# Decoder layer, second phase: turning the normalised tokens by VectorE blocks and transfers inside SBUF instead of TensorE transpositions

## The chip, the cores and the metric

One NeuronCore of a Trainium2 chip runs the whole program. It has five engines with queues of their own: TensorE (PE, and PEld for its weight loads), VectorE (DVE), ScalarE (ACT), GpSimd (POOL) and SyncE (SP), which here issues nearly all transfers. Engines wait for each other by semaphores only, and each works through its queue in order. The metric is the device time of one execution in microseconds; less is better.

## What is computed

Tokens are 4096 rows (16 sequences of 256) of 256 features. Three layers follow each other, each a sublayer, a residual sum and a layer norm:

```
x = _layernorm(x + attn(x, ...), axis=-1)           # first phase
x = _layernorm(x + xattn(x, ctx, ctx, ...), axis=-1)  # second phase
x = _layernorm(x + ffn(x, ...), axis=-1)            # third phase
```

The second one, which the change touches, is a differential attention over the context with 16 heads of 16 features:

```
s1 = einsum('bshe,bthe->bhst', q1, k1) / scale ;  s2 = einsum('bshe,bthe->bhst', q2, k2) / scale
attn = softmax(s1) - gain * softmax(s2)
o = einsum('bhst,bthe->bshe', attn, vp) ; o = (o - mean) / sqrt(var + EPS)
out = o.reshape(B, S, D) @ wo.T
```

where q1 and q2 are linear in the normalised tokens x. The queries therefore need x with features on partitions, while the first phase leaves it in X1 with tokens on partitions.

## The kernel before

All matrices are 32-bit floats. Where precision matters a value is split into a high and a low part.

**Blocks.** `phase_b` handles the tokens in 8 groups p of 512 (two sequences) and each group in two halves c of 128 features (8 heads). One such half is a block B = 2p + c; there are 16 (`NB`). A block has two units u = 2B + b, one per sequence; there are 32 (`NU`). A unit takes eight steps s, two for each of the four pairs of heads i, so there are 256 steps (`NS`), of which 16 make a block. Preparations run ahead: steps start at -52, beside the end of phase a.

**One step on TensorE** (`step` in `tensor`, L1340): `maxima(s + 14)`, the raw scores of a unit 14 steps ahead, whose maximum VectorE takes (L1495, one reduction a step); `scores(s)`, the same scores again with rows of minus maximum added through four extra partitions; on even steps `values`, the product with the values; and then what `due` puts on that step: `rows` (L1239) turns the maxima, `turn_o` (L1277) and `turn_n` (L1285) turn outputs, `prep_k` and `prep_v` make keys and values of later blocks, `prep_x` (L1209) turns tokens. `scores(s)` waits until ScalarE has done exp of the step before (`act_ex`), since it writes the same banks P[4] and P[5].

**How x is turned.** `prep_x(B)` at step 16B - 41 makes four 128x128 transpositions of X1 into bank P[6]. A step later ScalarE copies the bank to the tile XF (L1407), and a step later GpSimd makes XS from XF by three instructions: the high part, the low part, the high part again (L1631 to L1635).

**Transfers.** SP's queue runs through the same steps. `load(B, i)` (L1100), at steps 16B - 23 + 3i, i = 0 to 3, brings the heads' keys from KS to KT and queries from XS to QT: 2 transfers of each, so 16 in a block. `put_maxima(u)` (L1120), at step 8u - 4, brings the turned maxima from NR into QT with two transfers; `scores` of step 8u waits for them through `d_mr`. `load_ctx` brings context for two blocks. Modulo 16, the steps on SP are: 9 load i = 0; 12 put_maxima, load_ctx, load i = 1; 15 load i = 2; 2 load i = 3; 4 put_maxima. All transfers go through the helper `dma` (L118, shown as L119).

The order of the work is fixed by these step numbers; nothing is chosen while it runs.

Of the kernel before, what the change touches and what calls it, by code (L numbers as in the profile page):

```python
# [6 lines left out]
ALU = mybir.AluOpType  # L7
# [90 lines left out]
def due(step, first, every, count):  # L98

    k, r = divmod(step - first, every)  # L100
    return k if r == 0 and 0 <= k < count else None


def f32(ap):
    return ap.bitcast(F32)
# [12 lines left out]
def dma(e, o, i, sem):  # L118
    e.dma_start(o, i).then_inc(sem, 16)  # L119
# [759 lines left out]


LEAD = 14
NU = 4 * NP
NB = 2 * NP
NS = 8 * NU
# [5 lines left out]
def phase_b(M, a_end):  # L890
    nc, a, P, PP, X1, ident, nhalf = M.nc, M.a, M.P, M.PP, M.X1, M.ident, M.nhalf
    put = Place(M, 0)
# [4 lines left out]
    XF = put("XF", [128, TOK])  # L897
# [17 lines left out]
    put = Place(M, M.spare)  # L915
# [12 lines left out]
    ZR = put("ZR", [128, 2, 4, 2])  # L928
    VM = put("VM", [128, 16])
    VR = put("VR", [128, 16])  # L930
    BN = put("BNb", [128, 4, 6])
    AG = put("AGb", [128, 4, 2])
    RS = put("RSb", [128, 4])
# [25 lines left out]
    d_cr = M.sem("b_cr")  # L959
    d_ld = [[M.sem(f"b_ld{i}_{h}") for h in range(4)] for i in range(2)]  # L960
    d_mr = [M.sem(f"b_mr{i}") for i in range(2)]
    d_T = M.sem("b_T")
    d_V = M.sem("b_V")
    pe_g = M.sem("b_pe_g")
# [13 lines left out]
    act_x = M.sem("b_act_x")  # L978
# [14 lines left out]
    dve_oh = M.sem("b_dve_oh")  # L993
    dve_x2 = M.sem("b_dve_x2")
    dve_ag = M.sem("b_dve_ag")
    dve_fold = M.sem("b_dve_fold")
    dve_seq = M.dve_seq
    pool_vt = M.sem("b_pool_vt")
# [2 lines left out]
    pool_xs = M.sem("b_pool_xs")  # L1001
# [29 lines left out]

    def x_due(s):
        return due(s, -41, 16, NB)

    def v_due(s):
        for i, at in enumerate((-17, -7, -3, -1)):
# [32 lines left out]
    def turn_n_due(s):  # L1069
        return due(s, 23, 8, NU)  # L1070

# [11 lines left out]
    def sync(e):  # L1083
        w = Passed(e)

        def load_ctx(p):
            w.wait_ge(pool_c, 4 * p)
            dma(e, CR[:, :, :], ctxT[:, :, p * TOK:(p + 1) * TOK], d_cr)

        def ones_rows(i):  # L1090
            w.wait_ge(dve_w, 5)
            if i:
                after(w, "w2")
            else:
                after_stack(w, 14)
            for g in range(2):
                dma(e, f32(KT[i][64 * g + 48:64 * g + 52, :, :, :]).rearrange("r i m t -> r i (m t)"),
                    f32(ones[:, :, :]).rearrange("r m t -> r (m t)").unsqueeze(1).to_broadcast([4, 4, 1024]), d_ones)

        def load(B, i):  # L1100
            p, c = B // 2, B % 2
            if B == 0:
                after_stack(w, 14)
                w.wait_ge(dve_w, 4)
                w.wait_ge(pe_g, 1)
            if B == 1:
                after(w, "w2")
            w.wait_ge(pool_ks, 2 * B + 2)
            w.wait_ge(dve_ks, 2 * B + 2)
            w.wait_ge(pe_st, 16 * (B - 2) + 8 + 2 * i + 2)  # L1110
            k, q = KT[B % 2], QT[B % 2]
            for g in range(2):
                h = 2 * i + g
                dma(e, f32(k[64 * g:64 * g + 48, i, :, :]).rearrange("r m t -> r (m t)"),
                    f32(KS[16 * h:16 * h + 16, c, :, :, :]).rearrange("d l m t -> d (l m t)"), d_ld[B % 2][i])
                if B:
                    w.wait_ge(pool_xs, 3 * B + 3)
                    dma(e, f32(q[64 * g:64 * g + 48, i, :, :]).rearrange("r b t -> r (b t)"), f32(XS[16 * h:16 * h + 16, c, :, :]), d_ld[B % 2][i])

        def put_maxima(u):  # L1120
            q, b = QT[u // 2 % 2], u % 2
            w.wait_ge(act_nr, u + 1)
            w.wait_ge(pe_st, 8 * (u - 4) + 8)
            for g in range(2):
                dma(e, f32(q[64 * g + 48:64 * g + 52, :, b, :]), f32(NR[u % 2][16 * g:16 * g + 16, :]), d_mr[u % 2])

        def load_fold():
            for i in range(4):
                w.wait_ge(d_ld[0][i], 64 * NP)
                w.wait_ge(d_ld[1][i], 64 * NP)  # L1130
            w.wait_ge(pe_v, 4 * NP)
            for name in T:
                dma(e, T[name], a[name].rearrange("(c p) n -> p c n", c=2), d_T)
            w.wait_ge(d_ones, 80)
            for o, name in ((vb, "vb"), (vc, "vc"), (v2, "v2"), (br[:, :, :], "br"), (cols[:, :], "cols")):
                dma(e, o, a[name], d_V)
            dma(e, BC[:, 0, :], a["BC"][:, 0, :], d_V)

        def first_queries():
            w.wait_ge(dve_w, 4)  # L1140
            w.wait_ge(pe_g, 1)
            w.wait_ge(pool_xs, 3)
            for i in range(4):
                for g in range(2):
                    h = 2 * i + g
                    dma(e, f32(QT[0][64 * g:64 * g + 48, i, :, :]).rearrange("r b t -> r (b t)"), f32(XS[16 * h:16 * h + 16, 0, :, :]), d_ld[0][i])

        def first(i):
            if i == 0:
                load_ctx(0)  # L1150
            elif i == 1:
                dma(e, bd[:, :, :, :], a["bdw"], d_w)
            else:
                dma(e, wor[:, :, :], a["xwoT"].rearrange("(c p) n -> p c n", c=2), d_w)
                dma(e, kones[:, :], a["kones"], d_ones)

        def step(s):
            if s == -33:
                first_queries()
            u = due(s, -4, 8, NU)  # L1160
            if u is not None:
                put_maxima(u)
            p = ctx_due(s)
            if p is not None:
                load_ctx(p)
            for i in range(4):
                B = due(s, 3 * i - 23, 16, NB)
                if B is not None:
                    load(B, i)
            for i, at in enumerate((-16, -6)):  # L1170
                if s == at:
                    ones_rows(i)
            if s == NS - 28:
                load_fold()

        return first, step

    def tensor(e):
        w = Passed(e)
# [160 lines left out]
        def step(s):  # L1340
            busy(BUSY.get(s, 0))
            if 0 <= s + LEAD < NS:
                maxima(s + LEAD)
            if s in (0, 1):
                busy(2, 4 + 2 * s)
            if 0 <= s < NS:
                scores(s)
            v = values_due(s)
            if v is not None:
                values(v)  # L1350
            u = rows_due(s)
            if u is not None:
                rows(u)
            o = turn_o_due(s)
            if o is not None:
                turn_o(*o)
            u = turn_n_due(s)
            if u is not None:
                turn_n(u)
            k = k_due(s)  # L1360
            if k is not None:
                prep_k(*k)
            B = x_due(s)
            if B is not None:
                prep_x(B)
            v = v_due(s)
            if v is not None:
                prep_v(*v)
            o = out_due(s)
            if o is not None:  # L1370
                output(*o)
            f = fold_due(s)
            if f is not None:
                fold(f)
# [3 lines left out]
    def scalar(e):  # L1378
        w = Passed(e)
# [10 lines left out]
        def step(s):  # L1390
            v = values_due(s - 1)
# [9 lines left out]
                w.wait_ge(d_mr[u % 2], 32 * (u // 2))  # L1401
                e.activation(NR[u % 2][:, :], low[0:32, :], ACT.Copy).then_inc(act_nr, 1)
            B = x_due(s - 1)
            if B is not None:
                w.wait_ge(pe_x, B + 1)
                w.wait_ge(pool_xs, 3 * B)
                e.activation(XF[:, :], P[6], ACT.Copy).then_inc(act_x, 1)  # L1407
            v = v_due(s - 1)
            if v is not None:
                p, i = v  # L1410
# [5 lines left out]
            if u is not None:  # L1416
                p, c, b = u // 4, u // 2 % 2, u % 2
# [4 lines left out]
            k = k_due(s - 1)  # L1422
            if k is not None:
                B, m = k
# [17 lines left out]
    def vector(e):  # L1442
        w = Passed(e)
# [28 lines left out]
        def step(s):  # L1472
            o = out_due(s - 1)
            if o is not None:
                p, b, halves = o
# [43 lines left out]
            if s == -26:  # L1519
                w.wait_ge(d_ones, 16)  # L1520
                e.tensor_copy(ones[:, :, :], kones[:, :].unsqueeze(2).to_broadcast([4, 2, TOK])).then_inc(dve_w, 1)
            u = turn_n_due(s - 1)
            if u is not None:
                c, b = u // 2 % 2, u % 2
# [53 lines left out]
    def gpsimd(e):  # L1578
# [27 lines left out]
        def step(s):  # L1606
# [16 lines left out]
            B = x_due(s - 2)  # L1623
            if B is not None:
                xs = XS[:, B % 2, :, :]
                w.wait_ge(act_x, B + 1)
                for i in range(4):
                    w.wait_ge(d_ld[B % 2][i], 64 * ((B - 2) // 2 + 1))
                after_stack(w, 13)
                one.wait()  # L1630
                one.done(e.tensor_copy(xs[:, 0, :], XF[:, :]), pool_xs)  # L1631
                one.wait()
                one.done(e.tensor_tensor(xs[:, 1, :], XF[:, :], f32(xs[:, 0, :]), ALU.subtract), pool_xs)
                one.wait()
                one.done(e.tensor_copy(xs[:, 2, :], f32(xs[:, 0, :])), pool_xs)  # L1635
            u = due(s, 11, 8, NU)
# [931 lines left out]
```

## Time and profile before

| | us |
|---|---|
| median of 3 runs | 1552.7 |
| lowest, highest | 1552.16, 1553.82 |
| span of the profiled execution | 1550.1 |
| TensorE busy in it | 1502.6 (97%) |
| VectorE, ScalarE, GpSimd busy | 1139.4, 847.5, 372.8 |

The profile shows one execution. The first phase fills it to about 350 us, the second one, between about 350 and 820 us, is the one in question, and the third follows. The span is 2.6 us below the median of the times. Times in rows are counted from the span's start. A matmul's own duration is modelled, and matmuls overlap, so the distance between the starts of two rows says what TensorE spent on the first. The clock column (PEclk) is the granted share of TensorE's 2.4 GHz: 0.50 is its other level, 1.2 GHz. A row of SP is the time that it took to issue a transfer, not the transfer.

### The profile page before, as it was taken

How to read it: one execution, taken by the hardware profiler on the slowest of the kernel's cores; microseconds unless marked ns; L12 is line 12 of the kernel's file. 1: busy time of each engine (PE TensorE's matmuls, PEld its weight loads, DVE VectorE, ACT ScalarE, POOL GpSimd, SP SyncE). 2: the span in 40 equal slices, each digit the busy share in tenths (PEclk: the TensorE clock that was granted, in tenths of full speed). 3: DMA queues.
4: the chain of work that ended last, by engine and by line, in shares of the span. 5: the costliest groups of instructions: out<-in, count | busy, mean ns of one | idle time of the engine just before them, and what ended most of it. 6: DMA issues, size and time to landing. Idle time of an engine off the chain costs nothing.

```text
span 1550.1 us, 28824 instructions
## 1 busy us (share of the span) xinstructions
PE 1502.6 (97%) x11288; PEld 1065.1 (69%) x11288; DVE 1139.4 (74%) x2305; ACT 847.5 (55%) x1123; POOL 372.8 (24%) x404
## 2 busy tenths in 40 slices
PE   8999999899999999999999999999999999999998
PEld 4333333335566666666656898888989898888887
DVE  6445555548799999999967877777676767777675
ACT  5888889876688888888863421222222221222221
POOL 1000000124556667666453300000000000000000
PEclk9999999999899999999999999999999999999999
DMA  7656665446565666657652100000000000000000
GB/s 153 137 112 117 122 121 103 71 95 113 95 93 88 105 89 98 110 78 96 93 169 69 62 1 15 1 14 1 1 15 1 14 1 15 1 15 1 1 14 14
DMA packets 61576, 97.37 MB, mean 63 GB/s; under 512 B 12461, under 2 KB 29881, under 8 KB 61441
## 3 DMA queue, kind: packets, MB, share of 16 engines
q1 hardware_dynamic: 61312, 95.34, 33.3%
q8 instruction: 89, 1.46, 0.4%
q14 instruction: 47, 0.38, 0.1%
q10 hardware_dynamic: 128, 0.20, 0.0%
HBM read 26.29 MB, written 4.19 MB: 20 GB/s over the span
## 4 chain that ended last, share of the span: by engine, by line
PE 84%; DVE 8%; ACT 3%; SPq 3%; issue 2%; DMA 1%; POOLq 0%; DVEq 0%; POOL 0%; ACTq 0%
PE ps L109 79%; SPq L119 3%; PE ps L1277 2%; DVE NM L1495 2%; ACT H L614 1%; ACT PX L1438 1%; DVE EE L758 1%; PE ps L1239 1%; DVE XC L2106 1%; PE ps L1285 1%; PE ps L1914 0%; DMA ST<-QS 0%; PE ps L1905 0%; PE ps L1209 0%; DVE QS L678 0%
## 5 line engine op out<-in xcount | busy, mean ns | idle before, releaser
L1495 DVE TENSOR_REDUCE NM<-ps 128x4 f32<-128x1024 f32 x256 | 307.5, 1219 | 29.2 <-PE ps L109 27.7
L1438 ACT ACTIVATE PX<-ps 128x1024 f32<-128x1024 f32 x256 | 262.2, 1024 | 80.2 <-PE ps L109 79.0
L614 ACT ACTIVATE H<-ps,b1c 128x1024 f32<-128x1024 f32 x256 | 268.2, 1118 | 48.6 <-PE ps L109 47.0
L2066 ACT ACTIVATE GF<-ps,cols 128x512 f32<-128x512 f32 x128 | 88.2, 689 | 295.7 <-PE ps L109 295.6
L109 PE MATMUL ps<-XC,W_sw_w 128*128 128x512 f32 x768 | 185.8, 393 | 0.0
L2257 DVE CAST GH<-GF 128x512 fp32r<-128x512 f32 x192 | 82.0, 427 | 106.9 <-ACT GF L2066 101.8
L109 PEld LDWEIGHTS ps<-XC,W_sw_w 128*128 128x128 f32 x768 | 140.5, 188 | 28.0
L2365 POOL TENSOR_SCALAR RSc<-AGc 128x4 f32<-128x4 f32 x23 | 6.9, 298 | 599.5 <-DVE AGc L2152 599.5
L109 PE MATMUL ps<-PX,VT 128*32 128x256 f32 x2048 | 138.6, 388 | 0.1
L2259 DVE TENSOR_TENSOR GH<-GF,GH 128x512 fp32r<-128x512 f32 x192 | 133.2, 694 | 6.6
L109 PE MATMUL ps<-KT,QT 48*128 48x512 f32 x512 | 128.1, 498 | 3.7 <-DVE NM L1495 1.8
L2061 ACT ACTIVATE GF<-ps 128x512 f32<-128x512 f32 x64 | 38.0, 596 | 169.2 <-PE ps L109 169.2
L109 PE MATMUL ps<-H,w2p 128*32 128x512 f32 x1024 | 124.8, 605 | 3.0 <-ACT XF L1407 1.1
L109 PE MATMUL ps<-QT,KT 52*128 52x256 f32 x1024 | 109.2, 290 | 4.7 <-ACT PX L1438 3.8
L109 PEld LDWEIGHTS ps<-QT,KT 52*128 52x128 f32 x1024 | 90.1, 187 | 26.1 <-ACT PX L1438 10.7
L109 PE MATMUL ps<-W_ml_w,GH 128*128 128x256 f32 x768 | 103.6, 285 | 0.2
L758 DVE TENSOR_SCALAR EE<-ps,b2p 128x512 f32<-128x512 f32 x63 | 47.1, 747 | 77.0 <-PE ps L109 76.9
L109 PEld LDWEIGHTS ps<-KT,QT 48*128 48x128 f32 x512 | 47.8, 184 | 80.7 <-issue 60.2
L109 PEld LDWEIGHTS ps<-W_sw_w,GH 128*128 128x128 f32 x768 | 100.0, 191 | 4.5
L109 PE MATMUL ps<-W_sw_w,GH 128*128 128x256 f32 x768 | 102.7, 283 | 0.0
L109 PEld LDWEIGHTS ps<-W_ml_w,GH 128*128 128x128 f32 x768 | 98.0, 191 | 5.8 <-issue 3.4
L109 PE MATMUL ps<-ST,w1s 48*128 48x512 f32 x512 | 96.5, 451 | 5.3 <-ACT H L614 2.0
(240 smaller groups left out, 2560.3 us busy)
## 6 DMA issues: line engine op xcount, KB each, us to landing
KT<-KS SPq DMA_DIRECT2D x128, 192.0 KB, 4.7
ST<-QS SPq DMA_DIRECT2D x254, 96.0 KB, 2.8
QT<-XSb SPq DMA_DIRECT2D x128, 96.0 KB, 4.2
XT<-in_xT_dram SPq DMA_DIRECT2D x8, 512.0 KB, 4.1
raw_a<-in_x_dram SPq DMA_DIRECT2D x8, 512.0 KB, 4.3
CR<-in_ctxT_dram SPq DMA_DIRECT2D x8, 512.0 KB, 4.7
out_dram<-X SPq DMA_DIRECT2D x7, 512.0 KB, 2.9
R_sw_w<-in_sw_w_dram SPq DMA_DIRECT2D x6, 512.0 KB, 5.5
```

What stands on the lines that cost most here:

```text
L109: return e.matmul(o, l, r, start=start, stop=stop, skip_group_check=True)
L119: e.dma_start(o, i).then_inc(sem, 16)
L614: e.activation(H1[s % 8][:, :, :], PP[s % 3][:, :, :], ACT.Tanh, bias=b1c[:, half:half + 1], scale=1.0).then_inc(act_th, 1)
L758: e.tensor_scalar(EE[:, j % 4, :], P[6][:, :], b2p[:, 0:1], None, ALU.add).then_inc(dve_ee, 1)
L1239: t = e.transpose(low[0:32, 128 * qc:128 * qc + 128], f32(NS2[u % 2][:, 4 * qc:4 * qc + 4, :, :]).rearrange("p g l n -> p (g l n)"), ident)
L1277: t = e.transpose(P[7][:, 256 * qc + 128 * i:256 * qc + 128 * i + 128], OT[f][:, i, 128 * qc:128 * qc + 128], ident)
L1438: e.activation(PX[s % 3][:, :, :, :], PP[2][:, :, :].rearrange("p g (c q) -> p g c q", c=2), ACT.Exp, bias=0.0, scale=0.25).then_inc(act_e ...
L1495: e.tensor_reduce(NM[u % 2][:, qc, :, :, i], PP[qc][:, :, :].rearrange("p g (m k) -> p g m k", m=2), AX.X, ALU.max, negate=True).then_inc( ...
L2061: e.activation(g[:, :], o, ACT.Silu, bias=0.0, scale=1.0).then_inc(act_g, 1)
L2066: e.activation(g[:, :], o, f, bias=cols[:, col:col + 1], scale=1.0).then_inc(act_g, 1)
L2257: e.tensor_copy(h[:, 0, :], g[:, :]).then_inc(dve_h, 1)
L2259: e.tensor_tensor(h[:, 1, :], g[:, :], f32(h[:, 0, :]), ALU.subtract).then_inc(dve_h, 1)
```

## The change

For blocks 0 and 1 nothing changes (`X_FIRST` = 2). For blocks 2 to 15:

- TensorE's four transpositions and ScalarE's copy of the bank to XF go.
- VectorE, at step 16B - 50, turns the 32x32 blocks of the 128 features of four token tiles in one instruction, from X1 to a new tile TX of 128 x 512. It waits for the transfers that read TX the time before.
- A turned 32x32 block still sits at the wrong place. Four groups a of four transfers, at steps 16B - 48 + a on SP, each carry 32 partitions x 512 bytes (16 KB) from TX to their place in XF; that is 16 transfers for a block. The first one waits for VectorE's instruction and for GpSimd's last reading of XF.
- GpSimd waits for them instead of for ScalarE, and reads XF with the token order unpicked (four dimensions in place of one). It makes the same three instructions.
- A scratch buffer that this program doesn't use is set to 1024 bytes, which makes room for TX.

```
+            k = turn_x_due(s)                      # vector: due(s, 16 * X_FIRST - 50, 16, NB - X_FIRST)
+            if k is not None:
+                p, c = (k + X_FIRST) // 2, (k + X_FIRST) % 2
+                w.wait_ge(*a_end["nrm"](p))
+                w.wait_ge(d_xf, 256 * k)
+                e.transpose(TX[:, :, :, :].rearrange("p b v t -> p v b t"),
+                            X1[:, 4 * p:4 * p + 4, 128 * c:128 * c + 128].rearrange("p v (b t) -> p v b t", b=4)).then_inc(dve_xt, 1)
...
+        def turn_x(k, a):                          # sync
+            w.wait_ge(dve_xt, k + 1)
+            w.wait_ge(pool_xs, 3 * (k + X_FIRST))
+            for b in range(4):
+                dma(e, XF[32 * b:32 * b + 32, 128 * a:128 * a + 128], TX[32 * a:32 * a + 32, b, :, :].rearrange("p v t -> p (v t)"), d_xf)
...
+            for a in range(4):                     # sync, in step, behind the loads
+                k = turn_x_due(s - 2 - a)
+                if k is not None:
+                    turn_x(k, a)
...
             B = x_due(s)                           # tensor; scalar the same with s - 1
-            if B is not None:
+            if B is not None and B < X_FIRST:
                 prep_x(B)
...
-                w.wait_ge(act_x, B + 1)            # gpsimd
+                xf, hi, lo = XF[:, :], xs[:, 0, :], xs[:, 1, :]
+                if B < X_FIRST:
+                    w.wait_ge(act_x, B + 1)
+                else:
+                    w.wait_ge(d_xf, 256 * (B - X_FIRST + 1))
+                    xf = xf.rearrange("p (a v t) -> p a v t", a=4, v=4)
+                    hi, lo = (ap.rearrange("p (v a t) -> p a v t", v=4, a=4) for ap in (hi, lo))
...
-                one.done(e.tensor_copy(xs[:, 0, :], XF[:, :]), pool_xs)
+                one.done(e.tensor_copy(hi, xf), pool_xs)
...
-                one.done(e.tensor_tensor(xs[:, 1, :], XF[:, :], f32(xs[:, 0, :]), ALU.subtract), pool_xs)
+                one.done(e.tensor_tensor(lo, xf, f32(hi), ALU.subtract), pool_xs)
```

SP's queue in the middle of the phase, between steps 15 and 4 modulo 16, before (KT and QT are the destinations of the loads, NR the turned maxima; the first row is the start of load i = 2):

```order
L119 DMA KT<-KS 48x1x1024 [waits b_pe_st]
L119 DMA QT<-XSb 48x1x512
L119 DMA KT<-KS 48x1x1024
L119 DMA QT<-XSb 48x1x512
L119 DMA KT<-KS 48x1x1024 [waits b_pe_st]
L119 DMA QT<-XSb 48x1x512
L119 DMA KT<-KS 48x1x1024
L119 DMA QT<-XSb 48x1x512
L119 DMA QT<-NR 4x4x256 [waits b_act_nr]
L119 DMA QT<-NR 4x4x256
```

And the same stretch now:

```order
L119 DMA KT<-KS 48x1x1024 [waits b_pe_st]
L119 DMA QT<-XSb 48x1x512
L119 DMA KT<-KS 48x1x1024
L119 DMA QT<-XSb 48x1x512
L119 DMA XF<-TXb 32x128 [waits b_pool_xs,b_dve_xt]
L119 DMA XF<-TXb 32x128 x7
L119 DMA KT<-KS 48x1x1024 [waits b_pe_st]
L119 DMA QT<-XSb 48x1x512
L119 DMA KT<-KS 48x1x1024
L119 DMA QT<-XSb 48x1x512
L119 DMA XF<-TXb 32x128 x8
L119 DMA QT<-NR 4x4x256 [waits b_act_nr]
```

Sixteen transfers now stand in front of put_maxima, eight of them also in front of load i = 3.

TensorE's queue at steps 7 and 8 modulo 16, before (C holds the identity matrix; the maxima of step 8 are KT,QT, its scores QT,KT):

```order
L1285 MATMUL ps<-C,ON 128x128 [waits b_dve_pr,b_pool_on]
L1285 MATMUL ps<-C,ON 128x128
L1209 MATMUL ps<-C,X 128x128 [waits b_act_ot]
L1209 MATMUL ps<-C,X 128x128 x3
L109 MATMUL ps<-KT,QT 128x512 [waits b_dve_red,b_ld1_3]
L109 MATMUL ps<-KT,QT 128x512
L109 MATMUL ps<-QT,KT 128x256 [waits b_act_ex,b_mr1]
```

And now:

```order
L1304 MATMUL ps<-C,ON 128x128 [waits b_dve_pr,b_pool_on]
L1304 MATMUL ps<-C,ON 128x128
L109 MATMUL ps<-KT,QT 128x512 [waits b_dve_red,b_ld1_3]
L109 MATMUL ps<-KT,QT 128x512
L109 MATMUL ps<-QT,KT 128x256 [waits b_act_ex,b_mr1]
```

The four transpositions in front of step 8's maxima are gone; those maxima wait for load i = 3 (`b_ld1_3`) and its scores for put_maxima (`b_mr1`), as before.

VectorE's queue at steps 14 and 15 modulo 16, now:

```order
L1504 RECIPROCAL ZR<-ps 128x16 [waits b_pe_o]
L1508 TENSOR_TENSOR PR<-ps,ZR 128x2x128 [waits b_pool_oc,dve_seq]
L1514 TENSOR_REDUCE NM<-ps 128x4 [waits b_pe_max]
L1546 STREAM_TRANSPOSE TXb<-X 128x4x4x32 [waits b_xf]
L1514 TENSOR_REDUCE NM<-ps 128x4 [waits b_pe_max]
```

The instruction on L1546 is new and stands between two reductions of maxima; the others stood there in the same order.

## Rows read from the trace of the kernel before

**Rows 1.** Page, section 1: busy us, share of the span, instructions.

```profile
PE 1502.6 (97%) x11288; PEld 1065.1 (69%) x11288; DVE 1139.4 (74%) x2305; ACT 847.5 (55%) x1123; POOL 372.8 (24%) x404
```

**Rows 2.** Busy by stretch: length, engines' us (count), PEclk, DMA share, GB/s.

```profile
460.00:740.00 280.00, 277.06 (x2830) 182.40 (x2823) 258.63 (x401) 240.35 (x352) 178.19 (x181) 1.00 0.63 96
```

**Rows 3.** Timeline of TensorE, steps 7 and 8: start, us, what, count.

```profile
580.20 0.60 PE L1209 MATMUL ps<-C,X 128*128 128x128 f32 x4
580.73 0.50 PE L109 MATMUL ps<-KT,QT 48*128 48x512 f32 x2
581.20 0.50 PE L109 MATMUL ps<-QT,KT 52*128 52x256 f32 x4
```

**Rows 4.** Timeline of ScalarE there, exp of step 7.

```profile
580.03 1.02 ACT L1438 ACTIVATE PX<-ps 128x1024 f32<-128x1024 f32 x1 [0.17 <-PE ps L109]
```

**Rows 5.** Timeline of SP, steps 12 to 4: start, us of issue, what, count.

```profile
588.25 1.41 SPq L119 DMA_DIRECT2D QT<-NR  x2
...
590.19 0.62 SPq L119 DMA_DIRECT2D KT<-KS  x1
...
598.54 1.39 SPq L119 DMA_DIRECT2D KT<-KS  x1
...
603.07 2.08 SPq L119 DMA_DIRECT2D QT<-NR  x2
```

**Rows 6.** Timeline of TensorE, scores of step 8, one block later.

```profile
608.65 0.51 PE L109 MATMUL ps<-QT,KT 52*128 52x256 f32 x4
```

**Rows 7.** Timeline of SP, other places: prices of an issue.

```profile
23.58 1.20 SPq L119 DMA_DIRECT2D BO<-in_bo_dram  x4
267.31 1.21 SPq L119 DMA_DIRECT2D WS<-SM  x2
...
774.41 0.47 SPq L119 DMA_DIRECT2D FB<-in_ce_wvT_dram  x1
774.92 0.47 SPq L119 DMA_DIRECT2D FB<-in_ce_wo_dram  x1
```

**Rows 8.** Busy by stretch, columns as in 2: SP's burst.

```profile
590.00:603.00 13.00, 12.79 (x135) 8.49 (x135) 12.26 (x23) 11.32 (x18) 7.95 (x9) 1.00 0.87 153
```

**Rows 9.** A put_maxima issued with nothing else in flight: SP's timeline.

```profile
402.65 1.41 SPq L119 DMA_DIRECT2D QT<-NR  x2
```

**Rows 10.** The transfers of rows 9, by stretch, columns as in 2.

```profile
404.00:405.00 1.00, 0.90 (x11) 0.60 (x8) 1.00 (x3) 0.83 (x3) 0.52 (x1) 1.00 0.09 31
405.00:406.00 1.00, 1.00 (x8) 0.57 (x8) 1.00 (x2) 1.00 (x2) 0.00 (x0) 1.00 0.00 0
```

**Rows 11.** Timeline of SP around the first two blocks that change.

```profile
337.69 10.56 SPq L119 DMA_DIRECT2D KT<-KS  x3
...
371.77 2.12 SPq L119 DMA_DIRECT2D QT<-NR  x2
```

**Rows 12.** Timeline of TensorE, step 8.

```profile
375.10 0.50 PE L109 MATMUL ps<-KT,QT 48*128 48x512 f32 x2 [0.63 <-DMA QT<-XSb]
```

**Rows 13.** Clock after a gap on TensorE, by stretch, columns as in 2.

```profile
306.00:310.00 4.00, 1.23 (x19) 0.65 (x18) 3.50 (x10) 1.43 (x2) 0.00 (x0) 0.94 0.00 0
310.00:316.00 6.00, 6.00 (x26) 2.04 (x28) 1.00 (x3) 2.71 (x3) 2.50 (x3) 0.50 0.57 188
316.00:320.00 4.00, 4.00 (x27) 1.32 (x25) 1.41 (x3) 3.54 (x5) 0.61 (x1) 0.95 0.00 0
```

**Rows 14.** Timeline of TensorE, scores two steps apart, at the lower clock.

```profile
395.47 0.63 PE L109 MATMUL ps<-QT,KT 52*128 52x256 f32 x4
...
400.68 0.63 PE L109 MATMUL ps<-QT,KT 52*128 52x256 f32 x4
```

**Rows 15.** VectorE, groups of instructions: count, busy us, mean ns, idle before.

```profile
L2257 DVE CAST GH<-GF 128x512 fp32r<-128x512 f32 x192 | 82.0, 427 | 106.9 <-ACT GF L2066 101.8
L2259 DVE TENSOR_TENSOR GH<-GF,GH 128x512 fp32r<-128x512 f32 x192 | 133.2, 694 | 6.6
```

**Rows 16.** The same view, stretch 460 to 740, the reduction.

```profile
L1495 DVE TENSOR_REDUCE NM<-ps 128x4 f32<-128x1024 f32 x161 | 194.0, 1220 | 14.7 <-PE ps L109 13.4
```

More of the change, by code:

```diff
@@ L881 @@
 LEAD = 14
+X_FIRST = 2
 NU = 4 * NP
@@ L930, in phase_b @@
     VR = put("VR", [128, 16])
+    TX = put("TXb", [128, 4, 4, 32])
     BN = put("BNb", [128, 4, 6])
@@ L961, in phase_b @@
     d_mr = [M.sem(f"b_mr{i}") for i in range(2)]
+    d_xf = M.sem("b_xf")
     d_T = M.sem("b_T")
@@ L995, in phase_b @@
     dve_ag = M.sem("b_dve_ag")
+    dve_xt = M.sem("b_dve_xt")
     dve_fold = M.sem("b_dve_fold")
@@ L1033, in x_due, with turn_x_due @@
         return due(s, -41, 16, NB)
+    def turn_x_due(s):
+        return due(s, 16 * X_FIRST - 50, 16, NB - X_FIRST)
     def v_due(s):
@@ L1403, in step @@
             B = x_due(s - 1)
-            if B is not None:
+            if B is not None and B < X_FIRST:
                 w.wait_ge(pe_x, B + 1)
@@ L2558 @@
     from concourse.bass_utils import run_bass_kernel_spmd
-    nc = bacc.Bacc("TRN2", target_bir_lowering=False, num_devices=1)
+    nc = bacc.Bacc("TRN2", target_bir_lowering=False, num_devices=1, dynamic_dma_scratch_size=1024)
     laid = layout(inputs)
```

## The prediction

> **What bounds the kernel now.** Start with the page's busy shares [rows 1]: TensorE is busy 97% of the span. Such a share says little of what one edit is worth, so look at the stretch where the change lies. From 460 to 740 us, ten blocks of the second phase, TensorE is busy 277.06 of 280 us, VectorE 258.63 (92%), ScalarE 240.35 (86%), at the full clock [rows 2]. Three engines are nearly full at once, and the binding one changes from step to step.
>
> At step 7 modulo 16 stand the four transpositions that the change removes. They take 0.53 us of TensorE's queue (start 580.20, next row 580.73 [rows 3]). But the scores behind them start at 581.20, and they need ScalarE's exp of step 7, which starts at 580.03 and takes 1.02, so ends at 581.05 [rows 4]. With or without the transpositions, these scores start at about 581.2. The removed work lies in the shadow of exp.
>
> Then look at the queue that the page hardly speaks of, SP's. Put_maxima of step 12 is issued at 588.25, the loads begin at 590.19, and the twelve transfers of loads i = 1 to 3 follow each other until put_maxima of step 4 is issued at 603.07 [rows 5]; that is 12.88 us for twelve, 1.07 each, without a pause. The scores of step 8 wait for this put_maxima and start at 608.65 [rows 6]. How soon could they? A put_maxima issued at 402.65 with nothing else in flight [rows 9] still has packets between 404 and 405 us and none from 405 to 406 [rows 10]: 2.35 us to the last packet, and I take 2.7 to the scores, for the semaphore. So of the 5.58 us between 603.07 and 608.65 only 2.9 are slack. **SP's queue is within 3 us per block of being what binds.**
>
> **What the change adds there.** Sixteen transfers for a block, all between put_maxima of step 12 and that of step 4, in a stretch where SP has no pause. The only question is what one costs SP. No row shows this transfer. The nearest by kind, SBUF to SBUF, 32 KB, and nothing of size before it, is WS<-SM: two in 1.21 us, 0.605 each [rows 7]. From below: four one-row transfers from DRAM in 1.20, 0.30 each; full ones from DRAM start 0.51 apart (774.41, 774.92) [rows 7]. From above: 1.07, the rate in the burst [rows 5], where the DMA engines are 87% busy [rows 8], so that issuing waits for them. The new transfers are 16 KB, against 192 and 96 for keys and queries, so they should let that queue drain rather than fill it. I take 0.605.
>
> One block, step by step: 16 x 0.605 = 9.7 us. Put_maxima is issued at 603.07 + 9.7 = 612.8, and the scores of step 8 start at 612.8 + 2.7 = 615.5 instead of 608.65: 6.8 us late. Nothing gives this back in the next block, since the chain is a ring: scores of step 8 (581.20), four steps to put_maxima of step 12 (588.25, 7.05 later), SP's burst (14.82, now 24.5), landing (2.7), scores of step 8 again: 34.3 in place of 27.45.
>
> Load i = 3 is late too, by eight transfers (4.8 us), and the maxima of step 8 wait for it; its last transfer is issued before the second eight, so it lands before put_maxima does and costs nothing of its own.
>
> Over the blocks:
> - Blocks 5 to 15: 11 x 6.8 = 75.
> - Block 3: put_maxima is at 371.77 [rows 11], and the maxima of step 8 already wait 0.63 us for a load until 375.10 [rows 12], so no slack: 371.77 + 9.7 + 2.7 = 384.2 against scores at about 375.6, 8.6.
> - Block 4 ran partly at the lower clock and so with more slack [rows 14]: half of 6.8, 3.4.
> - Block 2: its transfers fall among three of keys that are spread over 10.56 us [rows 11]. At 0.6 each those leave 8.7 free for 9.7: say 2 with what is pushed on.
>
> Together 89.
>
> **The clock.** From 306 to 310 us TensorE worked 1.23 of 4 us, and for the next six the granted clock was 0.50, the 1.2 GHz level, then 0.95 on average again [rows 13]. The new gaps are twice as long, once a block. At the lower level two steps took 400.68 - 395.47 = 5.21 us [rows 14], against 27.45 / 8 = 3.43. If the lower level holds for six us after a gap it costs 6 x 1.78 / 5.21 = 2.05; if part of it falls in the gap, less, down to none. I take 1.5 for each of 13 blocks: 20. These steps lie between scores of step 8 and put_maxima of step 12, in the ring, so nothing hides them.
>
> **What is taken at nothing.** TensorE's 14 x 0.53 = 7.4 us and ScalarE's 14 copies: hidden behind exp now, and behind SP's queue after; if that cover goes, they are a gain of up to 7. VectorE's new instruction writes 512 elements per partition: a cast of that size takes 0.43 and a subtraction 0.69 [rows 15], the reduction of 1024 takes 1.22 [rows 16]; so 0.4 to 1.2, I take 0.7, the nearer in kind being uncertain. Its cover is the 6.8 us in which TensorE, and then VectorE, stand still once a block; without it, VectorE has 21 us idle in 280 [rows 2], 2.1 a block. The reductions behind it start later, by at most its length, and TensorE's maxima two steps on wait for them. GpSimd's three instructions keep their count; read in four dimensions they may take longer, and no row shows by how much, from nothing to double; GpSimd is 36% idle [rows 2] and the load that needs XS comes a block later.
>
> The Trainium skill, page "VectorE: DVE Perf Modes", section "The three transpose paths", gives 311 ns for VectorE's turn of 128x128 in 16 bits. As an estimate from that page, four such tiles are 1.24 us, and 14 of them 17 us if VectorE were the bound. No run here shows the instruction yet.
>
> **Sum.** 89 + 20 = 109 on the span of 1550.1: 1659. The median of the runs lies 2.6 above the span, so 1662.
>
> **Rivals.**
> - *The burst's price.* Each new transfer costs SP 1.07, as keys and queries do, and the put_maxima behind them takes 0.7 longer. For it: the DMA engines are near full in the burst [rows 8], eight of the new ones follow directly on a load. Against it: their size. One block: 17.1 + 0.7, 14.9 late; 11 x 14.9 + 17 + 7.5 + 8 = 197, and 20 for the clock: 1770.
> - *Cheap transfers.* At 0.51 a block is 5.3 late: 58 + 7 + 3 + 1, and 15 for the clock, 1637. At 0.30 it is 1.9: 25, and 5 for the clock, 1583.
> - *The transfers are hidden, and nothing moves.* That needs less than 2.9 / 16 = 0.18 us for one; then exp binds at step 7 as before: 1552. No issue by SP in the rows is as short.
> - *Hidden, and TensorE gains.* As before, and exp is not what holds step 8, so that 13 x 0.53 = 7 us come back: 1546. The point from which it decides is the same 0.18.
> - *VectorE becomes the bound.* Transfers hidden, and 14 x 0.7 on an engine that is 92% busy: 1562. For it are the share and the 14.7 us that its reductions waited in 280 [rows 16]; against it, 2.1 us of slack a block.
>
> The rule for the two hidden ones stands in the Trainium skill, page "DMA: Bandwidth & Descriptors", section "Issuing engines are not separate DMA queues": the sequencer's time to start a DMA is usually small beside the DMA. By it the 16 issues would not count and the time would be 1546 to 1552; the rows speak against it here, since 0.6 us of issue times 36 in a block of 27.45 us is most of the queue.
>
> **How the numbers follow.** Forecast, one transfer at 0.45 to 0.7: 1662, own range 1625 to 1700, chance 0.62. Burst's price and what lies between, 1700 to 1775 and a little above: 0.19. Cheap, 0.2 to 0.45, with VectorE's case: 1560 to 1625, 0.11. Hidden and same: 0.04. Hidden and faster: 0.04. The range 1605 to 1745 holds the first, about half of the second and some of the third, 0.78. Slower by over 0.2% 0.92, within 0.2% (about what a measurement of this kernel can tell) 0.04, faster 0.04.
>
> **What the new profile would show.** SP's timeline: 16 rows XF<-TXb a block at about 0.6, put_maxima of step 4 issued some 10 us later behind step 12's than now. TensorE idle 6 to 7 us before scores or maxima of step 8, once a block, with a transfer into QT named as releaser. A block of 34 to 36 us in place of 27.45, the clock at 0.50 for some us after each gap. VectorE's busy share in the phase down to about 75%. The first phase and the third as before. I am wrong if SP's new rows are under 0.3 (then little moves), if they are over 0.9 (then 1700 and more), or if the gap comes before another step: then another chain was the nearer one.

## The result, and the profile after

| | before | after |
|---|---|---|
| median, us | 1552.4 (4 runs) | 1695.2 (4 runs) |
| lowest, highest | 1550.2, 1553.8 | 1691.7, 1697.6 |
| span of the profiled execution | 1550.1 | 1692.8 |
| mean granted clock in it | 0.993 | 0.941 |

The ratio is 1.092, with a 95% interval of 1.0905 to 1.0937: the changed kernel is 143 us slower. The forecast was 1662, range 1605 to 1745.

The page of the kernel after, section 1 (engine: busy us, share, instructions), beside [rows 1]:

```profile
PE 1543.2 (91%) x11232; PEld 1083.4 (64%) x11232; DVE 1150.2 (68%) x2319; ACT 841.3 (50%) x1109; POOL 373.0 (22%) x404
```

and section 4, the shares of the chain that ended last:

```profile
PE 72%; SPq 16%; DVE 5%; DMA 2%; issue 2%; ACT 2%; POOLq 0%; DVEq 0%; POOL 0%; ACTq 0%
```

TensorE has 56 instructions fewer and is busy 40.6 us longer, since part of its work now runs at the lower clock. SP's queue (SPq) makes 16% of the chain; in the kernel before it made 3%. The waits of TensorE between 350 and 950 us say whom it holds up (engine and line, what ended the wait: us in total, times, longest):

```profile
PE ps L109 <- DMA QT<-NR: 67.5, 13, 5.8
PE ps L109 <- DMA QT<-XSb: 32.3, 12, 4.9
PE ps L109 <- DMA KT<-KS: 5.8, 1, 5.8
```

Thirteen waits for put_maxima and twelve for the queries of load i = 3, about one of each in a block. The new tile's own rows say what the additions cost (duration of one in ns: lowest, median, highest; then first and last start in us):

```profile
L119 SPq DMA_DIRECT2D XF<-TXb x224: 515/591/2547, 339.0 to 855.2; - x112
L1546 DVE STREAM_TRANSPOSE TXb<-X x14: 699/700/702, 338.3 to 835.8; 128x512 f32<-128x512 f32 x14
```

One block on SP's timeline (start, us of issue, what, count), the counterpart of [rows 5]:

```profile
636.82 1.42 SPq L119 DMA_DIRECT2D QT<-NR  x2
...
646.64 6.03 SPq L119 DMA_DIRECT2D XF<-TXb  x8
652.71 0.59 SPq L119 DMA_DIRECT2D KT<-KS  x1
653.35 0.59 SPq L119 DMA_DIRECT2D QT<-XSb  x1
653.99 1.17 SPq L119 DMA_DIRECT2D KT<-KS  x1
655.21 0.97 SPq L119 DMA_DIRECT2D QT<-XSb  x1
656.22 6.11 SPq L119 DMA_DIRECT2D XF<-TXb  x8
662.37 1.40 SPq L119 DMA_DIRECT2D QT<-NR  x2
```

From put_maxima of step 12 to that of step 4 it takes 662.37 - 636.82 = 25.55 us, without a pause; before it took 14.82 in the block of rows 5. TensorE over the same stretch, the counterpart of [rows 6]:

```profile
657.06 0.44 PE L1304 MATMUL ps<-C,ON 128*128 128x128 f32 x2
659.53 0.50 PE L109 MATMUL ps<-KT,QT 48*128 48x512 f32 x2 [2.04 <-DMA QT<-XSb]
665.40 0.80 PE L109 MATMUL ps<-QT,KT 52*128 52x256 f32 x4 [5.37 <-DMA QT<-NR]
668.58 0.63 PE L109 MATMUL ps<-QT,KT 52*128 52x256 f32 x4
```

and its clock (columns as in rows 2: length, busy us of TensorE, its loads, VectorE, ScalarE, GpSimd, granted clock, DMA share, GB/s):

```profile
661.00:663.00 2.00, 0.00 (x0) 0.00 (x0) 0.63 (x2) 0.00 (x0) 1.78 (x3) 0.50 0.11 26
663.00:665.00 2.00, 0.00 (x0) 0.00 (x0) 0.00 (x0) 0.00 (x0) 1.76 (x3) 0.50 0.08 24
665.00:667.00 2.00, 1.60 (x16) 0.92 (x19) 0.00 (x0) 0.77 (x1) 1.69 (x2) 0.50 0.00 0
667.00:669.00 2.00, 2.00 (x18) 1.01 (x10) 0.17 (x1) 0.73 (x2) 0.00 (x0) 0.50 0.00 0
669.00:671.00 2.00, 2.00 (x14) 1.79 (x12) 1.92 (x5) 1.02 (x1) 0.00 (x0) 0.65 0.24 31
671.00:673.00 2.00, 2.00 (x27) 1.24 (x28) 1.65 (x2) 1.68 (x3) 0.74 (x1) 1.00 0.89 91
```

TensorE stands still from 660 to 665.4 us, and before its end so do VectorE and ScalarE. The clock falls to the 1.2 GHz level in the gap and TensorE works at that level for some five us behind the gap. In ten such blocks the granted clock over the first eight us behind these scores is 0.65 on the mean, between 0.50 and 0.76, which is 5.6 us at the lower level; in the kernel before it is 1.00 there in all ten.

**Where the 142.7 us of span went.** The issue time of each put_maxima works as a clock for the ring. Put_maxima(u) of the changed kernel is later than that of the kernel before by:

| | before | after | later by | added by |
|---|---|---|---|---|
| u = 0, step -4 | 354.10 | 361.86 | 7.8 | block 2: 7.8 |
| u = 1, step 4 | 371.77 | 391.85 | 20.1 | block 3: 12.3 |
| u = 3, step 20 | 402.65 | 430.73 | 28.1 | block 4: 8.0 |
| u = 5, step 36 | 432.88 | 468.88 | 36.0 | block 5: 7.9 |
| u = 25, step 196 | 714.20 | 855.79 | 141.6 | blocks 6 to 15: 105.6 |

Ten blocks take 28.13 us each before and 38.69 after, 10.56 more. Behind the last of the new transfers nothing more is lost. So the loss has the size and the place of SP's additions; what it consists of is for the experiments.

### The profile page after: what moved, and what is told of

It is laid out like the page before. It is cut to its first block, busy times and chain, and to the rows that moved or that the text cites. A ratio compares the mean times of both kernels' runs of the same rounds, so it can differ in the third digit from the quotient of the medians.

```text
span 1692.8 us, 28935 instructions
## 1 busy us (share of the span) xinstructions
PE 1543.2 (91%) x11232; PEld 1083.4 (64%) x11232; DVE 1150.2 (68%) x2319; ACT 841.3 (50%) x1109; POOL 373.0 (22%) x404
## 3 DMA queue, kind: packets, MB, share of 16 engines
q1 hardware_dynamic: 72064, 99.02, 31.6%
## 4 chain that ended last, share of the span: by engine, by line
PE 72%; SPq 16%; DVE 5%; DMA 2%; issue 2%; ACT 2%; POOLq 0%; DVEq 0%; POOL 0%; ACTq 0%
PE ps L109 69%; SPq L119 16%; DMA QT<-NR 2%; PE ps L1296 2%; ACT H L614 1%; DVE EE L758 1%; ACT PX L1457 1%; DVE XC L2138 1%; DVE NM L1514 0%; PE ps L1946 0%; DMA ST<-QS 0%; PE ps L1258 0%; PE ps L1937 0%; DVE QS L678 0%; DVE X L669 0%
## 5 line engine op out<-in xcount | busy, mean ns | idle before, releaser
L109 PE MATMUL ps<-QT,KT 52*128 52x256 f32 x1024 | 117.7, 309 | 71.3 <-DMA QT<-NR 67.5
L109 PE MATMUL ps<-KT,QT 48*128 48x512 f32 x512 | 138.4, 539 | 40.5 <-DMA QT<-XSb 32.3
L109 PEld LDWEIGHTS ps<-QT,KT 52*128 52x128 f32 x1024 | 98.6, 205 | 96.4 <-DMA QT<-NR 72.9
L109 PEld LDWEIGHTS ps<-XC,W_sw_w 128*128 128x128 f32 x768 | 141.6, 190 | 28.5
L109 PE MATMUL ps<-PX,VT 128*32 128x256 f32 x2048 | 151.7, 418 | 0.1
L109 PEld LDWEIGHTS ps<-KT,QT 48*128 48x128 f32 x512 | 51.6, 199 | 126.5 <-issue 71.2
L109 PE MATMUL ps<-XC,W_ml_w 128*128 128x512 f32 x384 | 99.2, 393 | 0.0
```

The source lines that it names most:

```text
L109: return e.matmul(o, l, r, start=start, stop=stop, skip_group_check=True)
```

## The experiments

Every kernel is the changed one with one edit, unless said otherwise. The kernels of experiments 2, 3, 4, 5 and 9 leave out a part of the turning: 32x32 blocks stay at the wrong places, or (in 5) half of XF isn't written. They show times, and are no replacements for the change. Its time is given as a median and as a ratio to the kernel before, run on the same chip, with its 95% interval; those runs of the kernel before had medians of 1550.2 to 1551.0.

### 1. The transfers alone

TensorE turns and ScalarE copies as before the change; VectorE's instruction is gone; SP sends 16 transfers of the same size in the same places, from X1 to TX, which nobody reads.

```
-            if B is not None and B < X_FIRST:      # tensor, and scalar
+            if B is not None:
                 prep_x(B)
...
-                dma(e, XF[32 * b:32 * b + 32, 128 * a:128 * a + 128], TX[32 * a:32 * a + 32, b, :, :].rearrange("p v t -> p (v t)"), d_xf)
+                dma(e, TX[32 * b:32 * b + 32, a, :, :].rearrange("p v t -> p (v t)"), X1[32 * a:32 * a + 32, 4 * p + b, 128 * c:128 * c + 128], d_xf)
```

> TensorE turns the tokens and ScalarE copies them for all blocks, as before; VectorE's new instruction is left out. SP still sends 16 transfers of 32 x 512 bytes a block at the same places, from X1 to TX, which nobody reads. Theory (the cost is 16 issues in front of put_maxima on SP's queue): all of it stays, 1685 to 1705, scores of step 8 waiting for QT<-NR some 5 us a block. Rival (part of the 143 us comes from VectorE's 0.70 us instruction or GpSimd's reading in four dimensions): clearly less, 1620 to 1670 if they carry a third or more.

Measured: 1688.4, ratio 1.0888 (1.0852 to 1.0923). All of the loss but some 5 us, for which the intervals overlap (1.0905 to 1.0937 for the change), is there with nothing but the transfers added, and with the same gap:

```profile
618.65 0.50 PE L109 MATMUL ps<-KT,QT 48*128 48x512 f32 x2 [2.20 <-DMA QT<-XSb]
624.32 0.80 PE L109 MATMUL ps<-QT,KT 52*128 52x256 f32 x4 [5.17 <-DMA QT<-NR]
```

### 2. The change without its transfers

GpSimd reads TX itself, so that everything but the 16 transfers is left.

```
-            for a in range(4):                     # sync
-                k = turn_x_due(s - 2 - a)
-                if k is not None:
-                    turn_x(k, a)
...
-                    w.wait_ge(d_xf, 256 * (B - X_FIRST + 1))   # gpsimd
+                    w.wait_ge(dve_xt, B - X_FIRST + 1)
+                    xf = TX[:, :, :, :]
```

> The changed kernel without the transfers: TensorE's transpositions and ScalarE's copies stay removed, VectorE's instruction stays, and GpSimd reads TX itself, so that the 32x32 blocks stand at wrong places. Theory (exp shadows the removed transpositions, VectorE has room): 1549 to 1555, no change. Rival one (TensorE gets 0.53 us a block back): 1543 to 1547. Rival two (VectorE was the hidden bound, 14 x 0.70 us): 1558 to 1563.

Measured: 1557.2, ratio 1.0042 (1.0021 to 1.0062), between two of the expected ranges. The rest of the change gains nothing. TensorE is free earlier at step 8 and waits for exp, as in the step from [rows 3] to [rows 4]:

```profile
583.93 0.51 PE L109 MATMUL ps<-KT,QT 48*128 48x512 f32 x2
584.84 0.50 PE L109 MATMUL ps<-QT,KT 52*128 52x256 f32 x4 [0.40 <-ACT PX L1453]
```

and over the stretch of [rows 2] its busy time falls by 4.8 us with ten blocks taking as long as before (28.24 us each against 28.13):

```profile
460.00:740.00 280.00, 272.25 (x2780) 177.56 (x2778) 261.61 (x410) 235.36 (x340) 178.20 (x181) 1.00 0.63 96
```

So what is lost here (3.9 us between the two profiled executions, 6.6 between the medians) is for the most part not lost in the ring. Put_maxima(5) is issued at 435.94 instead of 432.88; 3 us are gone before that, in the first blocks. The clock there was 0.57, where the kernel before has 1.00:

```profile
348.00:364.00 16.00, 15.39 (x48) 7.27 (x48) 10.25 (x12) 1.63 (x4) 3.44 (x5) 0.57 0.61 83
```

Just ahead of it stands a wait of 0.29 us, in the place in which TensorE had turned block 2 before the change:

```profile
349.55 0.63 PE L109 MATMUL ps<-KT,QT 48*128 48x512 f32 x2 [0.29 <-DVE NM L1510]
```

### 3. The same, but TensorE still turns block 2

```
-X_FIRST = 2
+X_FIRST = 3
```

> The second experiment again (no transfers, GpSimd reads TX, blocks at wrong places), but TensorE still turns block 2 as well, so that its filling of the steps before the first scores is as it was. Theory (3 to 4 of the 6.5 us there are a lower clock between 348 and 364 us, after a gap of 0.3 us that the removed transposition of block 2 opened): 1551 to 1554, the clock 1.00 in that stretch. Rival (VectorE's instruction costs all of it, 14 times 0.5 us): 1556 to 1558.

Measured: 1551.9, ratio 1.0002 (0.9977 to 1.0026). The clock stayed up:

```profile
348.00:364.00 16.00, 15.01 (x86) 7.64 (x88) 14.85 (x19) 4.67 (x8) 8.72 (x9) 1.00 0.68 93
```

The loss of experiment 2 is gone with the one block, and the thirteen turns of VectorE that remain cost nothing that can be measured. How much of this is the clock in one stretch is less sure. The two intervals (1.0021 to 1.0062, 0.9977 to 1.0026) just touch, and the twelve runs of this kernel spread from 1545.5 to 1563.5 us, with mean clocks from 0.997 down to 0.984, so the profiled one isn't all of them. In the traces the pattern holds: without the transpositions of block 2 the clock of 348 to 364 us is 0.50 to 0.57 in all ten kernels, nine of which also have new transfers; with them, and without new transfers, it is 1.00 in both. What the 0.29 us have to do with it isn't shown.

### 4. and 5. Count or bytes

Half the count with twice the bytes each (8 transfers of 32 x 1024 B, each to the partitions that it comes from), and the full count with half the bytes (16 of 32 x 256 B).

```
-            for b in range(4):
-                dma(e, XF[32 * b:32 * b + 32, 128 * a:128 * a + 128], TX[32 * a:32 * a + 32, b, :, :].rearrange("p v t -> p (v t)"), d_xf)
+            for j in range(2):
+                dma(e, XF[32 * a:32 * a + 32, 256 * j:256 * j + 256], TX[32 * a:32 * a + 32, 2 * j:2 * j + 2, :, :].rearrange("p b v t -> p (b v t)"), d_xf)
```

> 8 transfers of 32 x 1024 bytes a block in place of 16 of 32 x 512: the same bytes, half the count, two each at the same four places; the blocks stand at wrong places in XF. Theory (count of issues): SP's part falls from some 11.5 us a block to some 5.5, so 1610 to 1635. Rival (bytes, the DMA engines' time): 1685 to 1700.

Measured: 1624.2, ratio 1.0468 (1.0433 to 1.0503).

```
-                dma(e, XF[32 * b:32 * b + 32, 128 * a:128 * a + 128], TX[32 * a:32 * a + 32, b, :, :].rearrange("p v t -> p (v t)"), d_xf)
+                dma(e, XF[32 * b:32 * b + 32, 128 * a:128 * a + 64], TX[32 * a:32 * a + 32, b, 0:2, :].rearrange("p v t -> p (v t)"), d_xf)
```

> 16 transfers of 32 x 256 bytes a block in place of 32 x 512: half the bytes, the same count; half of XF isn't written. Theory (count): 1685 to 1700. Rival (bytes): 1610 to 1650.

Measured: 1695.8, ratio 1.0941 (1.0901 to 1.0980). The tile rows of the two, half count first:

```profile
L119 SPq DMA_DIRECT2D XF<-TXb x112: 542/620/2532, 338.9 to 783.3; - x112
```

```profile
L119 SPq DMA_DIRECT2D XF<-TXb x224: 519/591/2547, 336.5 to 852.1; - x112
```

Bytes cost nothing that was measured, the count costs all of it: half the count gave back 71 of 143 us. A transfer holds SP's queue about 0.6 us (median) whether a partition's part is 256, 512 or 1024 bytes.

### 6. What the clock costs

While it waits, TensorE makes 44 products of 256 columns into bank P[6] that nothing reads, 12 ahead of the maxima of step 8 and 32 ahead of its scores. The gap is still there, and the engine isn't idle in it.

```
+            gap = due(s, 8, 16, NB - X_FIRST - 1) is not None
+            if gap:
+                fill(12)
             busy(BUSY.get(s, 0))
             if 0 <= s + LEAD < NS:
                 maxima(s + LEAD)
+            if gap:
+                fill(32)
```

> The changed kernel, and in blocks 3 to 15 TensorE multiplies into its free bank P[6] at step 8, 12 products of 256 columns before that step's maxima and 32 between them and the scores: some 6 us of work at the full clock, inside the 8 to 9 us that it waits there. Nobody reads the products. Theory (a part of the loss is the lower clock after each gap: from the scores of step 8 to put_maxima of step 12 9.7 us in place of 7.05): the granted clock stays near 1.00 in the phase, these four steps return to 7.1 to 7.6, and 20 to 32 us come back: 1663 to 1675. Rival (those steps are long for another reason, or the filler only adds work): 1695 or more.

Measured: 1673.6, ratio 1.0789 (1.0753 to 1.0824). The mean clock is 0.979 in place of 0.941. Step 8 to put_maxima of step 12 took:

```profile
617.17 0.51 PE L109 MATMUL ps<-QT,KT 52*128 52x256 f32 x4
```

```profile
624.32 1.42 SPq L119 DMA_DIRECT2D QT<-NR  x2
```

7.15 us in this block. On the mean of ten blocks it is 7.18 before the change, 9.72 with it and 7.41 with the filler, of which one block, in which the clock fell all the same, took 10.09. So about 2.3 to 2.5 us of a block's 10.56 are the clock's. The block fell to 36.66 us, by 2.0: the scores start 0.2 us later behind put_maxima than without the filler, and SP's burst took 0.1 longer.

### 7. and 8. The transfers moved out of the burst

All 16 transfers at SP's steps 5 to 8, behind put_maxima of step 4.

```
-                k = turn_x_due(s - 2 - a)
+                k = turn_x_due(s - 7 - a)
```

> The changed kernel with its 16 transfers five steps later on SP, at steps 5 to 8, behind put_maxima of step 4, where SP stood idle for 5.8 us a block before the change, and ahead of load i = 0. Theory (what costs is SP's queue in front of put_maxima, and once that is mended SP's total of 20.5 + 9.7 to 12 us in a block of 28.1): 13 blocks of 30.2 to 32 us, 1575 to 1605. Rival (the transfers disturb the others wherever they stand): above 1650.

Measured: 1607.2, ratio 1.0365 (1.0324 to 1.0407), just above what was expected. No wait for put_maxima is left to speak of (1.0 us in all), yet a block takes 31.9 us, and SP's timeline says why: there is hardly a pause in it. In ten blocks SP has five pauses of over 0.15 us, 2.3 us together, where the kernel before has 8.2 us in a block on the mean.

```profile
604.90 1.41 SPq L119 DMA_DIRECT2D QT<-NR  x2
606.42 10.86 SPq L119 DMA_DIRECT2D XF<-TXb  x16
617.39 0.60 SPq L119 DMA_DIRECT2D KT<-KS  x1
...
620.95 2.20 SPq L119 DMA_DIRECT2D QT<-NR  x2
...
636.73 1.95 SPq L119 DMA_DIRECT2D QT<-NR  x2
```

In this form GpSimd also waited for XF:

```profile
POOL XSb L1663 <- DMA XF<-TXb: 48.9, 13, 7.1
```

A second run took most of that away (15.9 us in ten waits are left), by moving GpSimd's three instructions four steps later:

```
             B = x_due(s - 2)                       # gpsimd
+            if B is None or B >= X_FIRST:
+                B = x_due(s - 6)
+                if B is not None and B < X_FIRST:
+                    B = None
```

> The 16 transfers behind put_maxima as in the sixth experiment, and GpSimd makes XS of these blocks four steps later, at step 13, so that it no longer waits for them in front of its sum OC. Theory (SP's total of 31 us a block is what binds there): 1600 to 1608, no change, though GpSimd's wait goes. Rival (GpSimd's wait, handed on through OC to ScalarE and TensorE, carries part of the 57 us): 1575 to 1595.

Measured: 1602.6, ratio 1.0326 (1.0303 to 1.0350), with a block of 31.6 us. GpSimd's wait was worth some 5 us at most, and the two intervals overlap. SP's pauses of over 0.15 us come to 1.1 us in ten blocks. What binds is the sum of all that SP issues in a block, 29.8 us of its 31.6.

### 9. Moved, with half the count

The edit is the first one of 7 and 8 and the first one of 4 and 5 together: eight transfers of 32 x 1024 B a block, at SP's steps 5 to 8.

```
-                k = turn_x_due(s - 2 - a)
+                k = turn_x_due(s - 7 - a)
...
-            for b in range(4):
+            for j in range(2):
```

> 8 transfers of 32 x 1024 bytes in place of 16 of 32 x 512 (blocks at wrong places in XF), behind put_maxima of step 4, at steps 5 to 8. SP then has 20.5 + 5.5 = 26 us of issues in a block of 28.1. Theory (the count on SP's queue decides, and below its length nothing shows): 1553 to 1566. Rival (SBUF to SBUF transfers disturb the others by their bytes): 1590 or more, near the 1607 of sixteen transfers at the same place.

Measured: 1558.4, ratio 1.0045 (1.0031 to 1.0059), the same as experiment 2, which has no transfers at all. A block takes 28.2 us in both. TensorE waits for none of the transfers into QT in 460 to 740 us, and SP's timeline has pauses again, such as the one from 614.5 to 615.3:

```profile
607.51 1.90 SPq L119 DMA_DIRECT2D QT<-NR  x2
609.51 5.00 SPq L119 DMA_DIRECT2D XF<-TXb  x8
615.32 0.60 SPq L119 DMA_DIRECT2D KT<-KS  x1
```

Eight take 5.00 us here, 0.63 each (up to 5.91 in other blocks), with put_maxima ahead of them and no load.

Beside experiment 4 this parts two conditions. SP issues for about 24 us of a block in both, less than the 28.1 of a block before the change, so neither asks for more than the queue can issue. With the eight in front of put_maxima, inside the ring, the time is 1624.2; with the same eight behind it, 1558.4. So room on the queue isn't enough; the new transfers must also stand behind what the ring waits for. Sixteen don't fit even there (experiments 7 and 8).

### 10. and 11. Put_maxima through ScalarE's queue

ScalarE makes NR itself, so it could send it at once, with the new transfers where the change puts them (first) and moved as in 7 (second).

```
-            u = due(s, -4, 8, NU)                  # sync
-            if u is not None:
-                put_maxima(u)
...
                 e.activation(NR[u % 2][:, :], low[0:32, :], ACT.Copy).then_inc(act_nr, 1)   # scalar
+                q, b = QT[u // 2 % 2], u % 2
+                w.wait_ge(act_nr, u + 1)
+                w.wait_ge(pe_st, 8 * (u - 4) + 8)
+                for g in range(2):
+                    dma(e, f32(q[64 * g + 48:64 * g + 52, :, b, :]), f32(NR[u % 2][16 * g:16 * g + 16, :]), d_mr[u % 2])
```

> The changed kernel, but ScalarE issues put_maxima, right behind its copy to NR, so that it no longer stands behind the 16 transfers. Load i = 3 still stands behind eight of them. Theory: no wait on QT<-NR; SP has some 17 + 12 = 29 us of issues a block, and TensorE waits for QT<-XSb before the maxima of step 8 as now (2 to 4 us) or a little longer: 1580 to 1620. Rival (the loads, not put_maxima, carry the delay): above 1660.

Measured: 1642.8, ratio 1.0593 (1.0532 to 1.0654). TensorE no longer waits for put_maxima, and for the queries only 1.3 us in all, but for exp 47.3 us, in 46 waits.

> Both: the 16 transfers at steps 5 to 8 and put_maxima issued by ScalarE. SP has 17 + 9.7 = 26.7 us of issues in a block of 28.1, ScalarE four issues more in a block of which it is idle 3.9 us. Theory: SP's queue is hidden again and the time is that of the kernel without transfers, 1555 to 1565. Rival (ScalarE's issues come into its chain of exp, four times 0.6 us a block): 1580 to 1590.

Measured: 1626.2, ratio 1.0485 (1.0440 to 1.0530), slower than with put_maxima left on SP (1607.2). Both expectations missed, and ScalarE's timeline of the second shows what they had left out:

```profile
594.96 2.18 ACTq L119 DMA_DIRECT2D QT<-NR  x2
597.35 0.60 ACT L1449 ACTIVATE KS<-ps 128x512 fp32r<-128x512 f32 x1 [2.42 <-issue]
597.84 1.02 ACT L1459 ACTIVATE PX<-ps 128x1024 f32<-128x1024 f32 x1
```

The two issues hold ScalarE's queue for 2.18 us, and the exp behind them is late; TensorE's scores, which need exp of the step before, start behind it:

```profile
598.91 0.55 PE L109 MATMUL ps<-QT,KT 52*128 52x256 f32 x4 [2.10 <-ACT PX L1459]
```

TensorE waited for exp 45 us in all, 47 times, with no wait for put_maxima; in the kernel of experiment 7 the waits for exp are 18.1 us in all, 20 times. An issue cost its engine time on either queue, and here it was moved from one nearly full queue to another.

No version with the new way of turning was found that beats the kernel before, and experiments 2 and 3 say why none was to be expected: with the transfers free, the ratio is 1.000 to 1.004.

## Why the prediction was right, point by point

**The shadow of exp: right.** Experiment 2 shows the scores of step 8 waiting 0.40 us for exp where the transpositions stood. TensorE's 7.4 us were worth nothing, as far as a spread of a few us can tell.

**SP as what becomes the bound, and its ring: right.** Experiments 1 and 2 part the change in two, and the transfers have all of the loss but the few us of experiment 2. That the late put_maxima is never made good is shown by the table of the ring: it grows in block after block, by 10.6 us on the mean of ten.

**One transfer at 0.605: too low for the burst.** By itself the price is as taken: 0.591 in the middle, 0.63 from start to start. But each group of eight stands behind a load, and takes 5.9 to 7.5 us, 0.77 for one on the mean. The first one is dear in every group of eight, 1.2 to 1.5 us, as the tile's row for the eight of 656.22 says:

```profile
L119 SPq DMA_DIRECT2D XF<-TXb x8: 516/590/1385, 656.2 to 661.7; - x8
```

The first one waits, as I read it, for what the load has put in the queues; no run tests that by itself, but where no load stands ahead the first takes 0.57 on the mean (experiments 7, 8 and 9). So 16 took about 12.2, some of it given back by a shorter issue of load i = 3, and put_maxima of step 12 to that of step 4 grew by 11.5 us (14.42 to 25.93, means of ten blocks), not by 9.7. The bound from above, 1.07, was too high, though not for the reason given, the sizes: half the bytes changed nothing (experiment 5).

**The slack of 2.9: too low.** The one block that was read has 5.58 us from put_maxima to scores; ten blocks have 6.53 on the mean, and about every second one has 7.1. After the change it is 3.04, near the 2.7 taken for the landing. So 3.5 us were slack. A mean over blocks would have served better than one.

**The clock at 1.5 for a block: too low.** Step 8 to put_maxima of step 12 grew by 2.5 us (7.18 to 9.72, means of ten blocks), and experiment 6 took 2.3 of it back. The six us at the lower level were about right, 5.6 behind the gap; of the level's time before that, some falls in the gap. What was too low is the share of that time that is lost: 1.78 of 5.21 from [rows 14], 0.34, where 2.5 of 5.6 is 0.45. And the 2.05 that this gave as the upper end was taken down to 1.5 for a part in the gap, while the gap hides none of these 5.6.

Together, for ten blocks: 11.5 + 2.5 - 3.5 = 10.5 a block (10.56 before rounding), against a forecast of 9.7 + 1.5 - 2.9 = 8.3. A block takes 38.7 us, which lies outside the 34 to 36 named as a sign.

**The start-up: too low.** Block 2 cost 7.8 where 2 was said, block 3 12.3 where 8.6, block 4 8.0 where 3.4; 28 against 14, and 17 with the clock's share. The transfers of block 2 were compared with the time free on SP, but not with who waits for the keys behind them: the first four took 2.46 us, the next four 5.50, the keys between and behind them came late, and TensorE stood still for one of its longest waits (the longest is 5.80),

```profile
353.46 0.80 PE L109 MATMUL ps<-KT,QT 48*128 48x512 f32 x2 [5.79 <-DMA KT<-KS]
```

and then ran at the lower level:

```profile
348.00:364.00 16.00, 10.54 (x29) 5.46 (x30) 7.96 (x9) 0.76 (x2) 2.51 (x3) 0.55 0.49 76
```

Part of that fall is there without any transfer (experiment 2), which nothing in the prediction allowed for.

The sum again: start-up 28.1, block 5 7.9, ten blocks 105.6, makes 141.6, against 109. Every cost was too low, which the slack, too low as well, made up for in a small part; none was of the wrong kind. The measured time lies 33 us above the forecast, near the upper end of the range given to it, 1700.

**Load i = 3 at no cost of its own: right.** Its queries end waits of 32.3 us in all. But each lies ahead of a wait for put_maxima, which SP issues eight transfers later, and the sum of the ring above leaves nothing over for it.

**VectorE's instruction at 0.7, GpSimd at nothing: right.** It takes 0.700 each time. The Trainium skill, page "VectorE: DVE Perf Modes", section "The three transpose paths", led to an estimate of 1.24 for four tiles. The measured 0.700 for 128x512 in 32 bits is little more than half of it, and the measurement decides. GpSimd's three instructions take 0.61, 1.27 and 0.61 us with four dimensions, where they took 0.61, 1.28 and 0.61 with one:

```profile
L1663 POOL CAST XSb<-XF x7: 611/611/611, 470.4 to 702.0; 128x512 fp32r<-128x512 f32 x7
```

**The rivals.** The burst's price and the cheap transfers fall with the 0.591 of the tile's row and the 0.77 of the groups, which lies between the forecast's 0.605 and the burst's 1.07, nearer the first. The two hidden cases fall with experiments 1, 4 and 5. The rule that was named beside them is that of the Trainium skill, page "DMA: Bandwidth & Descriptors", section "Issuing engines are not separate DMA queues": the time to start a DMA is usually small beside the DMA. It doesn't help here: from issue to landing it is 1.8 us in the median, but landings overlap, and the 0.6 us of issue add up on the queue. VectorE as the bound falls with experiment 3. Its share in the changed kernel is 66% (52.93 of 80 us between 580 and 660), where 75% was forecast, since a block is longer than forecast.

## What to carry to other kernels

Count issues, not bytes, on the queue that issues the transfers, and ask two things before adding to it: does the queue have pauses for all of them in a round, and do they stand behind, not in front of, what the other engines wait for? With both, eight transfers of 32 KB cost nothing that was measured (experiment 9). In front of the awaited transfer the same eight cost some 73 us (experiment 4), though the queue had room; behind it, sixteen cost 57 (experiment 7), as it had none. Work taken from the busiest engine is worth something only where that engine is what ends last at that step. And when a ring gains a gap, price the lower clock behind it in full: a gap of 5.4 us was followed by five us and more at the lower level, all of it in the ring.

## What the runs showed of the hardware that was not expected

- With four transpositions fewer in a stretch with small gaps (experiment 2 against 3) the granted clock of the profiled executions is 0.57 in place of 1.00 over 16 us, and the median time is 5 us longer, though the program has less to do. The runs of either kernel spread over more than that.
- A put_maxima issued from ScalarE's queue holds it about as long as SP's (2.18 us for the two at 594.96; 1.3 to 2.2 on SP), and exp stands behind it.
- The length of a partition's part, 256 to 1024 bytes, hardly shows in the time of an issue: medians of 591, 591 and 620 ns in the burst, and 590 for 1024 bytes behind it (experiment 9).
